# Moving the second layer's first normalisation to VectorE, and tanh for one more gate

## Time and profile before

| what | value |
| --- | --- |
| median of 3 runs | 362.25 us |
| the profiled execution, its own time | 362.47 us |
| its span, first to last instruction | 360.7 us |
| PE busy | 349.0 us (97%) |
| DVE busy | 303.1 us (84%) |
| ACT busy | 299.8 us (83%), with 43 table loads of 1283 ns |
| POOL busy | 233.1 us (65%) |
| granted TensorE clock | 1.00 of full speed (2.4 GHz) in nearly all slices |

### The profile page before, as it was taken

How to read it: one execution, slowest core, us unless ns; L and a number is a source line. 1 busy time by engine, 2 the same in 40 slices (tenths; PEclk the granted TensorE clock), 3 DMA queues, 4 the chain that set the end, 5 groups by cost and what they waited for, 6 DMA issues and landing times.

```text
span 360.7 us, 5747 instructions
## 1 busy us (share of the span) xinstructions
PE 349.0 (97%) x1754; PEld 180.4 (50%) x1754; DVE 303.1 (84%) x516; ACT 299.8 (83%) x521; POOL 233.1 (65%) x296
## 2 busy tenths in 40 slices
PE   7999999999999999998999999999999999999996
PEld 4566544747565423433244447444455644464546
DVE  5889889978898885498899788999999999888950
ACT  4966876778679977999998889989999999589660
POOL 3266625314411602226999687999999999988990
PEclk9999999999999999999999999999999999999999
DMA  6268496571645303000000000000001000000000
GB/s 223 83 158 153 96 251 170 90 131 35 109 104 70 120 1 121 23 0 2 0 0 0 25 0 22 2 15 2 0 2 36 0 30 1 2 0 1 16 15 29
DMA packets 28942, 19.26 MB, mean 53 GB/s; under 512 B 4240, under 2 KB 27888, under 8 KB 28656
## 3 DMA queue, kind: packets, MB, share of 16 engines
q1 hardware_dynamic: 28912, 18.90, 22.5%
HBM read 13.32 MB, written 5.37 MB: 52 GB/s over the span
## 4 chain that ended last, share of the span: by engine, by line
PE 77%; ACT 12%; DVE 4%; issue 3%; POOL 2%; DMA 1%; ACTq 0%; DVEq 0%; POOLq 0%
PE bank L1028 13%; PE bank L1016 11%; PE bank L436 7%; PE bank L423 4%; PE bank L400 4%; PE bank L1099 4%; ACT da L1207 4%; PE bank L460 4%; PE bank L468 4%; PE bank L1005 4%; PE bank L1006 4%; PE bank L989 3%; PE bank L1052 3%; PE bank L1072 3%; ACT pt L631 3%
## 5 line engine op out<-in xcount | busy, mean ns | idle before, releaser
L1340 POOL TENSOR_TENSOR acc<-acc,hb 128x512 f32<-128x512 f32 x128 | 158.4, 1269 | 20.8 <-DVE hb L1284 20.6
L1284 DVE TENSOR_TENSOR_SCAN hb<-da,bank 128x512 f32<-128x512 f32 x128 | 146.3, 1201 | 13.9 <-PE bank L989 12.4
L681 DVE TENSOR_REDUCE mx<-bank 128x2 f32<-128x512 f32 x128 | 81.4, 680 | 9.9 <-PE bank L400 7.7
L1207 ACT ACTIVATE da<-dt,nega 128x510 f32<-128x510 f32 x128 | 81.7, 713 | 0.2
L1028 PE MATMUL bank<-gelu,ld 128*128 128x512 f32 x128 | 58.5, 593 | 1.1 <-ACT gelu L1195 1.0
L1016 PE MATMUL bank<-sil,ld 128*128 128x512 f32 x128 | 59.2, 592 | 0.0
L631 ACT ACTIVATE pt<-bank 128x512 f32<-128x512 f32 x72 | 39.7, 603 | 4.3 <-PE bank L423 2.7
L423 PE MATMUL bank<-q_st,k_st 51*128 51x512 bf16 (+1 forms) x128 | 39.0, 381 | 2.8 <-ACT pt L631 2.5
L1028 PEld LDWEIGHTS bank<-gelu,ld 128*128 128x128 f32 x128 | 24.0, 190 | 28.2 <-issue 27.2
L400 PE MATMUL bank<-k_st,q_st 48*128 48x256 bf16 x240 | 37.0, 272 | 0.4 <-DVE mx L681 0.2
L1016 PEld LDWEIGHTS bank<-sil,ld 128*128 128x128 f32 x128 | 23.6, 190 | 22.8 <-issue 22.0
(11 more groups left out here) (161 smaller groups left out, 540.5 us busy)
## 6 DMA issues: line engine op xcount, KB each, us to landing
q_st<-q_scr SPq DMA_DIRECT2D x15, 192.0 KB, 5.4
q_st<-q_scr SPq DMA_DIRECT2D x7, 384.0 KB, 5.0
ld<-in_pack SPq DMA_DIRECT2D x2, 1024.0 KB, 5.0
q_scr<-qk_parts SPq DMA_DIRECT2D x8, 192.0 KB, 3.9
k_st<-k_scr SPq DMA_DIRECT2D x14, 96.0 KB, 4.9
q_scr<-qk_parts SPq DMA_DIRECT2D x8, 128.0 KB, 2.6
out<-x SPq DMA_DIRECT2D x8, 128.0 KB, 1.9
ld<-in_pack SPq DMA_DIRECT2D x1, 968.0 KB, 7.5
```

The costliest lines, as they stand in the source:

```text
L681: eng.tensor_reduce(mx[:, 2 * pair:2 * pair + 2, q], score_bank(b, n)[:, :].rearrange("p (h k) -> p h k", h=2), AX.X, ALU.max).then_inc(mx ...
L1207: act(da(n)[:, :, 1:T], dt[:, g % 2, c, :].rearrange("p (b n) -> p b n", b=GB)[:, :, 1:T], ACT.Exp, scale=nega[:, c, s:s + 1]).then_inc(da ...
L1284: eng.tensor_tensor_scan(hb[:, s % NPAIR, c, :], da(n).rearrange("p b n -> p (b n)"), b_bank(g, s)[:, :], 0.0, ALU.mult, ALU.add).then_inc ...
L1340: TT(acc[:, g % 2, c, :], acc[:, g % 2, c, :], hb[:, s % NPAIR, c, :], ALU.add).then_inc(add_ok, 1)
```

## The change: what it does

1. `early_normalise` is new: DVE normalises groups 0 and 1 itself (four `tensor_scalar` each, subtract the mean, multiply by the reciprocal). ACT's `normalise` remains for groups 2 and 3, and POOL's `shifted` for the second part alone.
2. `TANH_X` takes in group 1: its two `gate_x` use tanh, and DVE gets two more `xm`. The halving of `dt`, `b_in` and `D` for that group follows from the same constant.
3. The first `hid` of group 0 waits for the last `pv` (`pv_ok`) where it waited for the last `residual`, and the first `y` waits for the last `heads` on PE (`ot_ps`).
4. The orders of all engines are new. The parts that the text speaks of are below: in the first layer `decay_rates` and `constants` come several batches earlier, and POOL's `ones` comes after its first `G` and `biased`.

```diff
-    scalar="""roots deviation0 xn_out deviation0 wide_out q_out own_keys normalised k_out normalised xn_out relu
...
-        3*E deviation 3*E o_out E normalise 3*E relu 2*E gate_exp E negated_maxima 2*E relu 2*E x_out decay_rates 3*E
-        taps 7*E gate_x E o_out 3*E sil 4*E negated_maxima E sil taps gate_z normalise E gate_x E b_in sil gate_z
-        o_out 2*dt D E x_out sil E 2*D taps E 2*D E taps E 2*D gate_x gate_z gate_x D E D b_in E D gate_z E 2*D E 2*D
-        E 3*D E D E D E 3*D E gelu o_out gelu 2*dt 3*D 2*gelu 7*D 2*hid deviation normalise hid x_out hid 2*taps
...
+        negated_maxima 6*E gate_exp 2*E decay_rates o_out 3*E q_out 2*E relu 2*E relu 2*E negated_maxima 2*E q_out
+        relu 2*E gate_exp relu 5*E gate_exp 4*E o_out 2*E negated_maxima E relu 2*E relu 3*E deviation 4*E o_out 2*E
+        gate_exp 2*E relu 3*E negated_maxima relu 2*E x_out 4*E taps 8*E o_out 4*E sil 4*E negated_maxima E gate_x sil
+        taps gate_z gate_x E sil b_in gate_z o_out E 2*dt D x_out D E sil taps E taps E 2*D E 5*D E gate_z 2*gate_x E
+        D E D gate_z b_in E 3*D E D E D E D E 5*D E D E gelu o_out gelu 3*D 2*dt 2*gelu 7*D 2*hid deviation normalise
...
-        mul conv clear residual conv scan zm scan zm 3*scan back_out scan residual scan clear heads scan back_out
-        4*scan residual statistics scan inverse1 2*scan 2*conv mul 2*zm mul 2*scan 2*mul 6*scan residual1 scan
...
+        M back_out gate_sum 3*M residual gate_norm 3*M gated statistics 3*M inverse1 early_normalise 3*M v_out M heads
+        M gate_sum back_out M gate_norm residual 4*M early_normalise 2*M gated 6*M conv 4*M heads mul clear_keys xm
+        mul conv zm clear xm mul zm heads back_out scan mul 2*conv scan zm 2*xm scan residual scan zm scan back_out
+        2*scan clear residual scan heads 2*scan back_out scan residual 2*scan statistics scan inverse1 2*scan 2*conv
...
-    gpsimd="""ones biased G split_k split_q 3*G shifted0 4*G split_q maxima_split 8*G biased split_k split_q
...
+    gpsimd="""G biased ones split_k split_q 2*G shifted0 5*G split_q maxima_split 8*G biased split_q maxima_split 8*G
...
-TANH_Z, TANH_X, TANH_FFN = (0, 1, 2, 3), (0,), (0,)
+TANH_Z, TANH_X, TANH_FFN = (0, 1, 2, 3), (0, 1), (0,)
...
+    EARLY_G = 2
...
         def normalise(g):
-            part = 0 if g < PARTS[0][1] // GTT else 1
             reached(eng, xT_ps, g - 2, 1, 1)
-            eng.wait_ge(nm_ok, 2 * part + 2)
+            eng.wait_ge(xn_ok, EARLY_G)
+            eng.wait_ge(nm_ok, 2)
...
             if g == 0:
-                settled(eng, done["x1_ok"], NB)
+                settled(eng, done["pv_ok"], 4 * NB)
             act(g3[:, c, :], f_bank(g, c)[:, :], ACT.Gelu, scale=t["h2s"][:, c:c + 1]).then_inc(g3_ok, 1)
...
+        def early_normalise(g):
+            eng.wait_ge(rs_ok, 1)
+            for q in range(GTT):
+                c = g * GTT + q
+                last = eng.tensor_scalar(xn[:, g % 2, q, :], x1[:, c, :], mv[:, c, 0:1], rstd[:, c:c + 1],
+                                         ALU.subtract, ALU.mult)
+            last.then_inc(xn_ok, 1)
...
             if g == 0:
-                settled(eng, done["x1_ok"], NB)
+                settled(eng, done["ot_ps"], NB)
             TT(y[:, c, :], acc[:, g % 2, c, :], zs[:, g % 2, c, :], ALU.mult).then_inc(y_ok, 1)
```

More of the change, by code:

```diff
@@ L72 @@
 ORDERS = dict(
[L73 to L96, removed]
@@ L121 @@
-    gpsimd="""ones biased G split_k split_q 3*G shifted0 4*G split_q maxima_split 8*G biased split_k split_q
[L122 to L125, removed]
+    sync="""x_in head x_in constants0 ffn_weights x_in put 3*put_keys 2*put fetch put 3*put_keys 2*put fetch stack
+        3*put 3*rows fetch stack put rows put loads put_keys rows put rows fetch 3*put loads stack rows 2*put_keys
+        2*rows fetch put stack 2*rows 2*put rows fetch stack 3*put 3*rows loads put fetch put stack put 3*rows fetch
+        stack loads 6*rows 4*b_rows 8*out landed""",
@@ new lines @@
+    scalar="""deviation0 roots xn_out deviation0 wide_out q_out 2*own_keys k_out relu 2*normalised xn_out normalised
+        2*xn_out own_keys k_out own_keys q_out deviation0 gate_exp relu normalised xn_out normalised q_out relu xn_out
+        normalised negated_maxima relu normalised gate_exp 2*xn_out 2*E k_out 3*E q_out 3*E negated_maxima relu 3*E
+        gate_exp relu 4*E q_out 6*E o_out 2*E q_out 2*E negated_maxima 5*E gate_exp 2*E o_out 5*E relu 3*E relu
+        negated_maxima 6*E gate_exp 2*E decay_rates o_out 3*E q_out 2*E relu 2*E relu 2*E negated_maxima 2*E q_out
[3 more added lines that the diff above has]
+        D E D gate_z b_in E 3*D E D E D E D E 5*D E D E gelu o_out gelu 3*D 2*dt 2*gelu 7*D 2*hid deviation normalise
+        hid x_out hid 2*taps sil gate_x sil gate_z gate_x 2*D gate_z b_in 2*D 2*sil 11*D normalise 10*D 4*gelu 2*dt D
+        x_out 3*D taps 4*D taps 7*D 4*hid gate_x sil gate_z gate_x sil gate_z D b_in 2*sil 17*D 2*gelu 2*D 2*gelu 2*dt
+        15*D 4*hid 2*sil D 2*sil 10*D gelu 5*D 3*gelu 4*D 4*hid""",
@@ new lines @@
+    vector="""clear_values ones moments inverse moments clear wide_q clear_values inverse first_split M v_out
+        first_split M moments 5*M inverse 2*M clear_values gate_sum M gate_norm M gated 8*M v_out 2*M gate_sum M
+        gate_norm 5*M gated 8*M v_out M clear_values M gate_sum gate_norm M gated 10*M heads 3*M v_out 4*M back_out
+        2*M residual 2*M heads 2*M back_out M gate_sum 2*M residual gate_norm 3*M gated 2*M v_out 5*M heads 3*M
+        gate_sum back_out 3*M gate_norm residual gated 4*M v_out 2*M gate_sum M gate_norm M gated 3*M v_out 5*M heads
+        M back_out gate_sum 3*M residual gate_norm 3*M gated statistics 3*M inverse1 early_normalise 3*M v_out M heads
+        M gate_sum back_out M gate_norm residual 4*M early_normalise 2*M gated 6*M conv 4*M heads mul clear_keys xm
+        mul conv zm clear xm mul zm heads back_out scan mul 2*conv scan zm 2*xm scan residual scan zm scan back_out
+        2*scan clear residual scan heads 2*scan back_out scan residual 2*scan statistics scan inverse1 2*scan 2*conv
+        2*mul zm scan zm scan 2*mul 7*scan 2*residual1 7*scan conv scan conv scan mul zm mul zm 3*scan 2*mul 2*scan
+        2*residual1 13*scan 2*mul 2*scan 2*mul 10*scan 4*residual1""",
@@ L126 @@
+    gpsimd="""G biased ones split_k split_q 2*G shifted0 5*G split_q maxima_split 8*G biased split_q maxima_split 8*G
+        split_k split_q maxima_split G biased 2*G constants 3*G split_q G maxima_split 5*G split_q 4*G maxima_split
+        12*G split_q G maxima_split 9*G maxima_split 2*G maxima_split split 2*start 5*add start 2*add split add start
+        18*add shifted 6*add 2*y 2*start 2*add split 30*add y 2*add y add 2*start 7*add split 25*add 2*y 29*add 2*y""",
 )
@@ L1225, in scalar_pieces @@
         return dict(
-            deviation=deviation, normalise=normalise, decay_rates=decay_rates, x_out=x_out, b_in=b_in,
+            deviation=deviation, normalise=lambda n: normalise(EARLY_G + n), decay_rates=decay_rates, x_out=x_out, b_in=b_in,
             sil=lambda n: ffn_silu(n // KC, n % KC),
@@ L1369, in constants @@
                               ALU.mult).then_inc(i_pool, 1)
-        return dict(constants=constants, split=split, shifted=shifted, start=lambda n: start_acc(n // CI, n % CI), add=lambda n: add(n // (2 * NS), n % (2 * NS)),
+        return dict(constants=constants, split=split, shifted=lambda n: shifted(1), start=lambda n: start_acc(n // CI, n % CI), add=lambda n: add(n // (2 * NS), n % (2 * NS)),
                     y=lambda n: gated(n // CI, n % CI))
```

43 lines of the change are left out of this document (23 added, 20 removed).

## The result

The changed kernel takes 359.96 us (median of five, 359.69 to 360.64), the kernel before 362.73 beside it (362.14 to 363.93). The ratio is 0.990, 95% interval 0.9866 to 0.9933. The profiled execution took 359.87 us with a span of 358.1, that is 2.6 us less than before.

The account below looks back on a forecast made before the run. ACT was taken to bound 147 to 199 us, PE alone after. Terms -2.57 - 1.03 + 0.63 + 0.6 = -2.4 us gave 359.9 us by the median (360.1 by the profiled execution), range 357.0 to 363.9.

Parts of the forecast that it names:

- Tanh, -2.57 us: ACT's group 1 gates: tanh removes two table loads of 1.28 us where ACT hardly waits, -2.57 us.
- The other order moves: Remaining order changes on all engines: 0, with 1 us to either side as an estimate.
- `b_in`, +0.6: ACT's `b_in` of group 1 waits for scan 1, `zm`, both `xm` and matmuls: +0.6 us, bounds 0 and 2.1.
- `xm` hidden on DVE: Two more `xm` between scans 1 and 2, 1.4 us together, hidden in DVE's waits for `b`: 0, bounds 0 and 1.4.
- One more `D`, +0.63: ACT before the first `gelu`: 23 decays come where 22 came, +0.63 us.
- `hid`, -1.03: ACT's idle time before `hid`'s table load goes by waiting for `pv` instead of the last residual: -1.03 us.
- Normalising on DVE, 0: Between 107 and 124 us ACT is relieved of 3.3 us, DVE gains 2.4: taken as 0, ends -2.4 and +2.4.
- rival E: DVE full from 107 us to group 0's last scan; `tensor_scalar` +2.4 and `xm` +1.4 show whole: 365.0, chance 0.12.
- `ones`, the fetch: POOL's three clears fit a gap; first fetch +0.5 us, covered by score tiles: 0, ends 0 and +0.5.
- B: First layer shortens too, ACT's 3.3 us at 107 to 124 us having set the pace: 358.0, chance 0.16.
- C: DVE or POOL sets the second layer's pace; only POOL's slack of 1.0 us is gained: 361.3, chance 0.24.
- D: Each `xm` runs in turn behind a POOL `add` of 1.25 us, 2.5 us between scans 1 and 2: 362.3, chance 0.08.

Follow-up runs that it names:

- e_hid: Kernel before with one wait changed: the first gelu of `hid` waits for `pv_ok` instead of `x1_ok`; 362.33 us, ratio 0.9949.
- e_nowait: Changed kernel with both narrowed waits (`hid`'s and the first `y`'s) put back to `x1_ok`; 359.95 us, ratio 0.9896 to the kernel before.
- e_early: Kernel before with the second layer's first two groups normalised on DVE instead of ACT, without POOL's `shifted(0)`; 364.88 us, ratio 1.0013.
- e_both: Kernel before with tanh for group 1's x gate, its two `xm`, and `hid` waiting on `pv_ok`, otherwise old orders; 365.17 us, ratio 1.0011.
- e_bothfix: Kernel before with tanh for group 1, `hid` on `pv_ok`, and three places of the old orders (DVE, ACT, PE) mended; 362.37 us, ratio 0.9963.
- e_tanh: Kernel before with tanh for group 1's x gate and two `xm`, `hid` still waiting on `x1_ok`, otherwise old orders; 367.50 us, ratio 1.006.
- e_port: Changed kernel with three more POOL adds of 128x512 released beside group 0's second `xm`; one execution, 359.81 us.
- e_notanh_nowait: Changed kernel without tanh for group 1 and its two `xm`, both waits on `x1_ok`; 364.12 us, ratio 0.9991 to the kernel before.
- e_nofill: The same kernel as e_notanh_nowait run again, for comparison with e_fill on one chip; 363.28 us.
- e_fill: The kernel of e_nofill with three extra PE matmuls, results overwritten, in the 2.75 us where PE stands still; 362.63 us, ratio 0.9975.

## Why the prediction was right, and where not

**The number and the sum.** The sum was -2.4 us against 2.6 in the spans, but the parts are not where the prediction put them. Behind the first scan it had all of the 2.4, and 1.8 came: 1.0 for the idle time ahead of `hid`, as in e_hid, and 0.8 for tanh with its orders where -2.57 + 0.6 + 0.63 = -1.3 was forecast. Ahead of the first scan it had nothing, and 0.8 came. That the two errors cancel is luck.

**What bounds.** Right for the kernel before: most of the gain lies in 147 to 199 us, and the rest follows by a fixed amount of PE work. But the prediction let ACT go on setting the pace. With the loads gone the chain runs through DVE and then PE.

**Tanh, -2.57 us.** The two loads are worth 2.5 us against the same orders without tanh (`hid`'s load at 196.95 for 194.53). What the prediction did not see is that this holds in the new orders alone. In the old ones the same edit cost 1.6 us, and against the old orders with the wait alone tanh and the new orders bring 0.8. The first step that failed is "The other order moves. [...] 0, with 1 us to either side": the orders bring nothing by themselves (ratio 0.9991), but they turn a loss into the gain. The working had the means, as the upper bound of 2.1 us for `b_in` assumed nothing hidden; that bound was even too low (3.25 in the old order).

**`b_in`, +0.6.** It waited 0.29 us on ACT. The new order's cover on ACT was counted rightly.

**`xm` hidden on DVE.** This is the second step that failed. They took 2.14 us, not 1.4, and they stand on the chain that ended last. The scans of states 1 and 2, first in the kernel before, then in the changed one:

```profile
162.19 2.32 DVE L1284 TENSOR_TENSOR_SCAN hb<-da,bank 128x512 f32<-128x512 f32 x2
...
165.61 2.33 DVE L1284 TENSOR_TENSOR_SCAN hb<-da,bank 128x512 f32<-128x512 f32 x2 [0.53 <-PE bank L989]
```

```profile
160.18 2.32 DVE L1291 TENSOR_TENSOR_SCAN hb<-da,bank 128x512 f32<-128x512 f32 x2
...
165.06 2.32 DVE L1291 TENSOR_TENSOR_SCAN hb<-da,bank 128x512 f32<-128x512 f32 x2
```

State 1 is 2.0 us earlier than before, state 2 only 0.55. No scan is later than before, because the new order had brought state 1 forward; about 1.5 us of that lead went to the `xm`.

**One more `D`, +0.63.** Right as a count: 33 stand between the first `D` and `hid` where 32 stood.

**`hid`, -1.03.** Right number, wrong cause. The idle time is gone, yet not by the wait: with the old wait the kernel takes the same 359.95 us. The residual moved to 190.68. The prediction noted that move and still paid the narrowing for it. Each of the two would do alone: e_hid shows the wait, e_nowait the order. (PE's idle time began at 198.26, behind a row of `b`, and not at 198.04 as the prediction reads it; nothing hangs on that.)

**Normalising on DVE, 0.** Right in the new orders, within 0.2 us. In the old ones the trace of e_early has it at 0.8 us, by rival E's mechanism for 0.6 of them.

**`ones`, the fetch.** The first fetch is issued at 15.51, half a microsecond later as said, with no effect on the end.

**Rivals.** B: the first layer does shorten, the first scan comes 0.8 us earlier. But orders and normalisation alone, with that same first scan, end at a span of 360.5, 0.2 under the kernel before, and B's 358.0 did not come. C: POOL's `y` came 3.9 us earlier and PE does not wait behind 199 us. D: its mechanism is real, its price was not: 0.2 to 0.8 us for one `xm` and nothing for the next, not 1.25 for each. DVE's waits for the rows of `b` took up a part of both `xm`; of the 4.9 us in the earlier trace rows this is left (1.4 of the 2.9 us that are gone lay ahead of the first scan):

```profile
DVE hb L1291 <- PE bank L988: 2.0, 4, 0.7
```

E: refuted by the first scan, which is 0.8 us earlier and not 2 later.

**The spread of the kernel before.** Where the kernel before took 362.5 to 367.2 us in 23 executions (median 364.34), e_nowait took 359.7 to 360.2 on the same chip, 4.4 us less and not 2.6. The forecast was made against an execution near the fast end of that spread. The traces show two disturbances in the first layer. In 2 of 6 profiled executions with the old orders (e_both, e_bothfix) the granted clock was at 0.97 in 40 to 80 us, ahead of all edits. In 2 others (e_hid, e_tanh) the matmuls between 6.6 and 10 us took nearly twice their time, though the profile grants 1.00 there. The same two matmuls in the kernel before and in e_hid:

```profile
7.46 0.62 PE L533 MATMUL bank<-xnT,head 128*32 128x256 f32 x2
```

```profile
8.59 1.06 PE L533 MATMUL bank<-xnT,head 128*32 128x256 f32 x2
```

By the first long group of score matmuls e_hid is 1.7 us behind (17.87 for 16.13 us), about its lag at the first scan. None of 8 executions with the new orders shows the clock's fall there, and by the same mark at the start they lie between 16.20 and 17.11 us. The new list of PE begins with nine of the sixteen `warm` (two matmuls each on constants) where the old one has seven, and PE does not idle ahead of the first transposes where it idled 0.3 us. That fits, but no run changed the `warm` alone, so the cause stays open.

## What to carry to other kernels

An edit that shortens one engine's queue is worth its price only if its new dependences have cover in the order: price the edit together with the place of what it makes wait, and test it in both orders. Then read the chain again, for another engine may set the pace once the queue is short. A removed wait and a moved producer can pay for the same idle time; count it once. Idle time of PE can cost more than its length: look at the granted clock behind it.

## What the runs showed of the hardware

An operation of DVE with both operands in SBUF and an operation of POOL that reads SBUF ran in turn: 0.90, 1.21 and 1.45 us for an `xm` of 0.69 (the 1.45 is 2.14 for two less one undisturbed), each ending 0.5 to 0.6 us behind POOL's operation. A clear on POOL, which only writes, stood beside the `xm` at 136.81 us in e_port, from 137.11 to 138.05, and added nothing: 0.91 us as against 0.90. The Trainium skill, page "SBUF — State Buffer", section "Who interferes with whom", states this lock, with write-only operations excepted; the trace agrees in both.

PE standing still for 2.3 and 2.75 us was followed, in some executions, by a stretch at half the clock that cost 1.4 to 2 us on top of the idle time. By the mean clock it was ten of twelve executions of e_notanh_nowait and six of twelve of e_nofill; with matmuls in the gap (e_fill), none of twelve had it.
